# Relative-position attention: scores released by pairs of heads, denominators one quad earlier, far-weight sum between two maxima

## What is computed

```python
# 32 batches, T = 100 queries, S = 361 keys, 16 heads of 16, MAX_REL = 32
q = query @ Wq + bq;  k = key @ Wk + bk;  v = value @ Wv + bv
attn1 = einsum('bhqd,bhkd->bhqk', rq, rk)
attn2 = einsum('bhqd,qkd->bhqk', rq, rel_k_table[_rel_idx(t, s)])   # clipped distance
attn  = softmax((attn1 + attn2) / scale)
w1 = einsum('bhqk,bhkd->bhqd', attn, rv)
w2 = einsum('bhqk,qkd->bhqd', attn, rel_v_table[_rel_idx(t, s)])
return (w1 + w2) @ Wo + bo
```

## Time and profile before

| quantity | value |
|---|---|
| median of 3 runs | 2763.64 us (2762.44 to 2764.74) |
| profiled execution: its time | 2754.06 us |
| profiled execution: its span | 2752.3 us |
| PE busy over the span | 2338.3 us (85%) |
| DVE busy | 1546.6 us (56%) |
| ACT busy | 1221.1 us (44%) |
| relative cross attention in the trace | about 1447 to 2329 us |

### The profile page before, as it was taken

The page is one execution under the profiler, slowest core; times in us unless marked ns, Lnnn a source line. Parts: engine busy times, 40 slices in busy tenths (PEclk is TensorE's granted clock), DMA queues, the critical chain, the costliest instruction groups (busy, mean ns, idle before and its releaser), DMA issues. The chain is left out here.

```text
span 2752.3 us, 53362 instructions
## 1 busy us (share of the span) xinstructions
PE 2338.3 (85%) x18240; PEld 1861.4 (68%) x18240; DVE 1546.6 (56%) x2929; ACT 1221.1 (44%) x2701; POOL 609.3 (22%) x682
## 2 busy tenths in 40 slices
PE   8989999778999999389957999999999996694047
PEld 5669999677999999277754666666666665452035
DVE  5866666583111111379963666666666665645865
ACT  2223333212434343156643565555555564436733
POOL 1101111155444444154431111121111210000000
PEclk9999999968999999689977999999999998797579
DMA  2223222183999999400006555455554552110211
GB/s 80 64 61 78 74 65 65 23 271 109 343 342 347 343 344 340 134 7 0 0 25 139 126 126 128 118 128 127 125 128 118 126 126 63 49 72 36 107 42 42
DMA packets 386450, 346.73 MB, mean 126 GB/s; under 512 B 70322, under 2 KB 364748, under 8 KB 384332
## 3 DMA queue, kind: packets, MB, share of 16 engines
q1 hardware_dynamic: 321612, 302.19, 36.7%
q10 hardware_dynamic: 52480, 26.83, 3.9%
q0 software_dynamic: 12288, 16.79, 2.8%
HBM read 258.72 MB, written 87.05 MB: 126 GB/s over the span
## 5 line engine op out<-in xcount | busy, mean ns | idle before, releaser
L2087 ACT COPY rel_probT<-rel_ps_t 121x400 f32<-121x400 f32 x384 | 196.8, 512 | 251.9 <-PE rel_ps_t L2319 251.9
L2099 ACT ACTIVATE rel_prob<-rel_ps_s,rel_nmx 100x361 f32<-100x361 f32 x512 | 264.9, 581 | 1.4 <-DVE rel_nmx L2201 1.4
L2319 PE MATMUL rel_ps_t<-rel_ident,rel_prob 100*121 100x100 f32 x1536 | 242.0, 280 | 7.3 <-ACT rel_probT L2087 7.3
L2319 PEld LDWEIGHTS rel_ps_t<-rel_ident,rel_prob 100*121 100x121 f32 x1536 | 195.6, 185 | 77.4 <-ACT rel_probT L2087 48.9
L1266 PEld LDWEIGHTS moe_ps_h<-moe_xeT,moe_w 128*128 128x128 f32 x2048 | 240.2, 193 | 5.1 <-issue 1.9
L1266 PE MATMUL moe_ps_h<-moe_xeT,moe_w 128*128 128x128 f32 x2048 | 240.7, 276 | 1.3 <-DVE moe_xeT L1431 1.3
L2201 DVE TENSOR_REDUCE rel_nmx<-rel_ps_s 100x2 f32<-100x722 f32 x256 | 232.8, 909 | 8.8
L1266 PE MATMUL moe_ps_y<-moe_w,moe_hT 128*128 128x256 f32 x1024 | 231.5, 379 | 0.0
L2832 PE MATMUL ffd_ps_y<-ffn_w_dT,ffd_oq 128*100 128x256 f32 x384 | 86.1, 386 | 145.7 <-DVE ffd_oq L2777 140.1
L1266 PEld LDWEIGHTS moe_ps_y<-moe_w,moe_hT 128*128 128x128 f32 x1024 | 189.6, 190 | 23.2
L1257 ACT ACTIVATE moe_hT<-moe_ps_h,moe_b 128x128 f32<-128x128 f32 x512 | 142.9, 376 | 137.4 <-PE moe_ps_h L1266 137.1
(11 more groups left out here) (427 smaller groups left out, 4958.7 us busy)
## 6 DMA issues: line engine op xcount, KB each, us to landing
moe_w<-in_L_ffn_w SPq DMA_DIRECT2D x128, 1024.0 KB, 9.6
rel_scores<-rel_r_ext SPq DMA_DIRECT2D x32, 818.8 KB
rel_r_key<-rel_scores SPq DMA_DIRECT2D x32, 818.8 KB
rel_weights<-rel_prob ACTq DMA_DIRECT2D x128, 204.7 KB
rel_by_dist<-rel_weights SPq DMA_DIRECT2D x32, 400.0 KB
mut_ctx_nat<-in_ctx SPq DMA_DIRECT2D x32, 363.0 KB
mut_ctx_T<-in_ctxT SPq DMA_DIRECT2D x16, 722.0 KB
rel_ctx_T<-in_ctxT SPq DMA_DIRECT2D x32, 361.0 KB, 3.4
```

The costliest lines, as they stand in the source:

```text
L2087: nc.scalar.copy(probT[:, pg % 2, c], ps_pT).then_inc(s_t_sb, 1)
L2099: last = nc.scalar.activation(prob[:, t.parity, slot, :], ps_s[0:S, j, 0:L], ACT.Exp, bias=nmx[:, slot:slot + 1])
L2319: last = nc.tensor.transpose(ps_pT[:, j, :], prob[:, pt.parity, QUAD * pg + j, c * STEP:c * STEP + R], ident[0:S, 0:S])
```

## The change

Four edits, all in `relative_cross`:

1. A semaphore `s_half` is raised after the exponentials of the first pair of a quad. `scores` of the next quad wait for `s_half` before heads 0 and 1, and for `s_p` only before heads 2 and 3.
2. In `JOBS` and `PLACES`, den moves from place 9 (quad 2) to place 6 (quad 1), r1 from place 6 to place 7, and v1 from place 8 to place 9. The numbers of den, r1 and v1 change with that, so the banks do too. Bank 0: xT, q, r0, den, v1, d1, v2; bank 1: k0, k1, v0, r1, d0, w2, out.
3. On DVE, `raw` is copied between the two maxima of quad 1, where it was behind both.
4. On DVE, the sum over far weights stands between the two maxima of quad 2, where it was at the end of quad 1.

```diff
+        s_half = sem("first_half_weights")
...
         JOBS = [("after", "xT"), ("next", "k0"), ("after", "q"), ("next", "k1"), ("after", "r0"), ("next", "v0"),
-                ("after", "r1"), ("next", "v1"), ("last", "den"), ("last", "d0"), ("last", "d1"), ("last", "w2"),
+                ("last", "den"), ("after", "r1"), ("next", "v1"), ("last", "d0"), ("last", "d1"), ("last", "w2"),
                 ("next", "v2"), ("last", "out")]
-        PLACES = [[0], [1], [2], [3], [4], [5], [6], [], [7], [8], [9, 10], [], [11], [12], [13], []]
+        PLACES = [[0], [1], [2], [3], [4], [5], [6], [7], [], [8], [9, 10], [], [11], [12], [13], []]
...
             act.sem_inc(s_p, 1)
+            act.sem_inc(s_half, 1)
...
-                if k == 1:
-                    last.then_inc(s_p, 1)
+                last.then_inc(s_p if k else s_half, 1)
...
                 for g in range(GROUPS):
                     maxima(t, g, 0)
-                    maxima(t, g, 1)
                     if g == 1 and prev.within(B):
                         dve.wait_ge(s_pv, GROUPS * prev.i + GROUPS)
                         nc.vector.tensor_copy(raw[:], ps_raw).then_inc(s_att, 1)
+                    if g == 2 and prev.within(B):
+                        dve.wait_ge(s_far, prev.i + 1)
+                        dve.wait_ge(s_pdist, 16 * prev.i + 16)
+                        nc.vector.reduce_sum(by_dist[:, :, 0], far[:], AX.X).then_inc(s_far_sum, 1)
+                    maxima(t, g, 1)
                     for k in range(4):
                         if g == GROUPS - 1 and k == 2:
                             normalise(t + 3)
                         empty(t, 4 * g + k)
-                    if g == 1 and prev.within(B):
-                        dve.wait_ge(s_far, prev.i + 1)
-                        dve.wait_ge(s_pdist, 16 * prev.i + 16)
-                        nc.vector.reduce_sum(by_dist[:, :, 0], far[:], AX.X).then_inc(s_far_sum, 1)
...
             def scores(t, g):
-                pe.wait_ge(s_p, GROUPS * t.i + (g + 1))
+                pe.wait_ge(s_half, GROUPS * t.i + (g + 1))
                 if g == 0:
                     pe.wait_ge(s_qh, t.i + 1)
                     wait_emptied(pe, t + -1, "k1")
                 for j in range(QUAD):
                     rows = slice(j * TILE, (j + 1) * TILE)
+                    if j == 2:
+                        pe.wait_ge(s_p, GROUPS * t.i + (g + 1))
                     last = mm(ps_s[0:S, j, 0:L], ...)
```

## The result

The changed kernel takes 2771.55 us, the median of 6 runs (2769.09 to 2776.99), against 2764.19 us before (6 runs, 2761.89 to 2768.0). The ratio is 1.0029 with a 95% interval of 1.0016 to 1.0042: slower by 7.4 us. That lies in the predicted range (2757 to 2774) and 5.5 us above the predicted 2766. The profiled execution took 2769.09 us, with a span of 2767.3; that of before took 2754.06, so these two differ by 15.0 us, more than the medians.

A forecast was written before the change was run, and what follows sets the result against it. The prediction took PE's work list as the bound: +0.33 at d1 less 0.25 at quad 0 gave +0.08 a turn, +2.1 us over 26 turns, even outside the loop; on the median 2763.64 it said 2766, range 2757 to 2774.

The forecast's parts named there:

- What bounds the kernel: Relative stage: PE, busy 569 of 605 us, sets the pace; only its standing, about 6%, can be won.
- Pairs, quad 0: Scores of quad 0, waiting by pairs: gain of 0.25 us a turn, between 0.19 and 0.29.
- Pairs, quads 1 to 3: The added wait in the middle of these scores: costs nothing, upper end 0.18 us a turn.
- r1 and den: Swap in quad 1: quad 2's scores lose their 0.25 us bracket but start 0.54 us later.
- Far sum: Between quad 2's maxima: d1, held by v1's emptying, starts 0.33 us later, bracket about 1.2 instead of 0.61.
- T2: The prediction's name for the start of scores in quad 2, 2013.25 before, 2013.79 forecast after.
- Sum of the loop: Loop turn: +0.33 - 0.25 = +0.08 us, times 26 turns = +2.1 us.
- case A: Three PE brackets go, one of about 1.2 us at d1 replaces them: 2766 us, 2760 to 2772; chance 0.6.
- rival B: Wait between heads 1 and 2 exposed in quads 1 and 3, +0.09 each: 2770; chance 0.28 including a 2780-or-above form.
- Outside the loop: Turns outside the loop, including +1.3 us for the far sum in the drain: even, give or take 2 us.

The follow-up runs named there:

- e1: Kernel before with only the waits by pairs (`s_half`, its increments, the two waits of `scores`); ratio 0.9985.
- e5: Kernel before with four further, already true waits for `s_p` between heads 1 and 2 of every quad; ratio 1.0043.
- e3: Changed kernel with the far sum put back at the end of quad 1; 2726.89 us, ratio 0.9879.
- e4: Kernel before with only the far sum moved between the two maxima of quad 2, den still at place 9; ratio 1.0148.
- e6: Changed kernel with v1 and r1 swapped in `JOBS`, v1 at place 7 and r1 at place 9; ratio 0.9984.
- e7: Changed kernel with four extra matmuls, their result never read, issued before the wait for d1's bank; ratio 1.0003.
- e2: Changed kernel without the waits by pairs: den, r1, v1, `raw` and far sum moved, scores wait as before; ratio 1.0077.
- e8: e2 with four extra matmuls, their result never read, issued before the wait for d1's bank; ratio 1.0019.

## Why the prediction was right, and what it missed

**What bounds the kernel.** PE's standing decides: right. Every kernel's turn moved with its brackets on PE.

**Pairs, quad 0.** Predicted 0.25 a turn, made of 0.19 for the two register waits and 0.06 for two heads being quicker than four. The next block after scores, the xT transposes, now starts at 2008.14, 0.84 behind the exponentials' end (2006.26 + 1.04 = 2007.30); before it started 2027.74 - 2026.71 = 1.03 behind the earlier trace rows, by this row of PE's timeline of before:

```profile
2027.74 0.39 PE L2251 MATMUL rel_ps_m<-rel_ident,rel_xn 100*128 100x100 f32 x2
```

So the gain in the shown turn is 0.19: the waits' part is there, the 0.06 is not. e1's turns, 0.23 shorter, bound the sum of all quads.

**Pairs, quads 1 to 3.** Predicted free: right. Scores of quad 1 still take 0.87, and in e5 four waits there take 0.87 too. In these runs a satisfied wait costs nothing where PE still has work in front of it; that its queue is the reason fits, and was not tested by itself.

**r1 and den.** Predicted start of quad 2's scores: 0.54 later after those of quad 1. Measured: 2020.50 - 2013.94 = 6.56 against 6.02, 0.54. The reciprocal ran where DVE had nothing to do, `raw` waited 0.34 and delayed no exponentials: right.

**Far sum.** Predicted d1 at T2 + 5.16, held by v1, and d0 a little behind the far sum. Measured 2025.66 - 2020.50 = 5.16, brackets 0.99 and 0.22. The bracket was to be about 1.2: d0 came at 3.63 instead of 3.54 behind the scores, and its transposes fill 0.54 of the time up to d1 and not 0.4. That moved no later block, since d1's start was right. e3, e4 and e6 show the parts: the far sum between the maxima costs 1.0 to 1.1 us a turn, the bank alone 0.2 while the far sum is there.

**Sum of the loop.** Predicted +0.08 a turn. Measured 26.47 - 26.36 = +0.11 in the typical pair. Over all 26 turns, falls left out, it is +0.10 or 2.5 us. This is case A.

**What was missing.** The sum took the granted clock of before, 1.00 in the loop, as given, though it had worked out that d1 would stand for 1.2 us in place of 0.61. Three falls at 1.6 us are 4.8 us. In the profiled executions the 26 turns of the loop take 693.05 us against 685.72, 7.3 longer: 4.8 by the falls and 2.5 by the turns. e7 shows what the falls hang on: with the 0.99 filled there are none, with the same turns, and the ratio is 1.0003. So the loop lost 7.3 us where the sum had 2.1. The measured time landed in the range partly by luck, for a reason that no case named: not rival B (e5), but A and a slower clock. That the loop's 7.3 is so near the 7.4 between the medians says little, since the profiled executions differ by 15.0 in all. How many falls the other five runs of the changed kernel had was not seen; their mean granted clock over the whole execution is 0.918 to 0.921, against 0.921 in the profiled one and 0.921 to 0.926 in e7's eleven runs.

**Outside the loop.** Predicted even, give or take 2 us. In the profiled executions it was not: from the last xT to the first instruction of the norm it is 94.65 us against 90.87, 3.8 longer, and from the first xT to the fourth 55.2 us against 52.4, 2.8 longer. Over the other kernels of this study these two stretches go from 90.1 to 98.4 and from 51.0 to 57.8 us, each profiled once. The windows of the last stretch, before and after:

```profile
2238.70:2329.57 90.87, 77.72 (x750) 56.62 (x746) 51.12 (x79) 46.75 (x103) 11.86 (x8) 0.92 0.33 76
```

```profile
2249.57:2344.22 94.65, 81.33 (x748) 59.33 (x746) 50.71 (x79) 47.31 (x103) 11.87 (x8) 0.89 0.32 74
```

PE is busy 3.6 us longer there with the same work, at a granted clock of 0.89 in place of 0.92: it is at half for about 21 us and not 14. So the clock goes with the 3.8 here too; no run isolates it outside the loop. The far sum behind the reciprocal, which I priced at 1.3, does show in the last turn: w2 starts 5.90 behind den (2337.54 - 2331.64) against 3.89 before (2323.44 - 2319.55), 2.0 later. But PE's idle time in the whole stretch is 13.3 us after and 13.2 before, so shorter waits elsewhere in it make up for that. The 2.8 us of the first stretch I don't attribute.

**Left open.** What exactly makes the clock fall in 3, 10 or 2 of the loop's turns is not settled. The changed kernel and e2 have the same brackets at d0 and d1 (0.22 and 0.99), but e2 also stands 0.44 before scores of quad 0, and falls 10 times instead of 3. e4 stands 0.73 and 0.75 close together and falls twice. Nearly every turn of these kernels has the same brackets, so they alone don't pick the turn. The three falls of the changed kernel stand six turns apart, so they are not scattered at random either. Shown is only that filling the 0.99 removed all falls of the loop, in one profiled execution each of e7 and e8.

## What to carry to other kernels

When a wait is taken away, follow the shared resource behind it: d1 waited for its PSUM bank, and the change only swapped which job had to be emptied first, behind a chain of DVE work that is 0.22 us shorter from the scores on and starts 0.54 us later. Put a long side job where its engine waits for others, not between two instructions that release others: the same 1.28 us sum costs 1.0 us a turn between the two maxima, and at the end of the quad before it delays the chain by 0.2 us. A bracket on TensorE can have a second price when it grows, the clock: 0.61 had none in the loop before, 0.99 had three falls. Look for turns of unequal length before explaining a few microseconds, and compare whole stretches, since the profiled executions here differed by 6.6 us in two stretches outside the loop.

## What the runs showed of the hardware

TensorE's granted clock fell to half for 3.4 us while it was working, 0.9 to 1.5 us after it had stood for 0.99 us, in 3 loop turns of 26, and in 10 of 26 when another 0.44 us bracket was in the turn; with 1.06 us of unread matmuls in that wait it did not fall in the loop. A semaphore wait whose value is worked out in a register costs PE 0.05 us behind a wait that blocked, and nothing behind queued matmuls. The Trainium skill, "TensorE: Matmul & The Clock Gate", section HAM oscillation — how this bites in real kernels, describes such falls for waits on DMA longer than these; the runs here show them behind waits of 0.99 us, and of 0.73 and 0.75 us close together.
